# Offsets of three rounds found in their own partitions, keys ahead of the early edge blocks, large searches moved into the rounds, x loaded behind the first block

## The reference

```python
def _L0_gnn_ref(node_features, edge_features, src, dst, W_node, b_node, W_edge, b_edge, W_msg, b_msg):
    h = node_features @ W_node.T + b_node
    e = edge_features @ W_edge.T + b_edge
    msg = h[src] + e
    msg = msg @ W_msg.T + b_msg
    n = node_features.shape[0]
    s = jax.ops.segment_sum(msg, dst, num_segments=n)
    deg = jax.ops.segment_sum(jnp.ones(dst.shape, msg.dtype), dst, num_segments=n)
    return s / jnp.maximum(deg, 1.0)[:, None]
x = _layernorm(x + _L0_gnn_ref(x, edge_attr_128, src, dst, ...), axis=-1)
```

## Time and profile before

| | |
|---|---|
| three runs, us | 789.67, 792.46, 793.79 (median 792.46) |
| the profiled execution's own time | 798.16 us |
| its span, first to last instruction | 796.4 us |
| mean granted TensorE clock | 0.981 |
| PE busy | 697.5 us, 88% |
| DVE, ACT, POOL busy | 613.5 us, 439.5 us, 258.6 us |
| DMA | 130.48 MB, mean 164 GB/s |

### The profile page before, as it was taken

The page is one execution under the profiler, slowest core; times in us unless marked ns, Lnnn a source line. Parts: engine busy times, 40 slices in busy tenths (PEclk is TensorE's granted clock), DMA queues, the critical chain, the costliest instruction groups (busy, mean ns, idle before and its releaser), DMA issues.

```text
span 796.4 us, 24735 instructions
## 1 busy us (share of the span) xinstructions
PE 697.5 (88%) x10331; PEld 622.1 (78%) x10331; DVE 613.5 (77%) x1120; ACT 439.5 (55%) x902; POOL 258.6 (32%) x205
## 2 busy tenths in 40 slices
PE   2624558999999899999999998999999999999995
PEld 2523446898898678988989887988889988989994
DVE  7507998799988668887888777789788788779822
ACT  4103955576565455655656554655656665656641
POOL 2112742000442714426416437353254443000000
PEclk9999969999999989999999999999999999999998
DMA  6985334363474255565563473744744564554200
GB/s 209 219 261 176 108 109 127 110 229 124 131 246 157 78 188 173 204 193 190 186 203 127 135 246 121 266 150 158 264 147 130 189 215 163 178 178 167 68 15 16
DMA packets 81030, 130.48 MB, mean 164 GB/s; under 512 B 11669, under 2 KB 24688, under 8 KB 80815
## 3 DMA queue, kind: packets, MB, share of 16 engines
q1 hardware_dynamic: 73214, 115.79, 43.9%
q0 software_dynamic: 6976, 12.16, 5.5%
q10 hardware_dynamic: 726, 0.90, 0.5%
HBM read 125.58 MB, written 3.23 MB: 162 GB/s over the span
## 4 chain that ended last, share of the span: by engine, by line
PE 65%; DVE 19%; issue 7%; DMA 4%; SPq 2%; DVEq 1%; another core or an unknown queue 1%; ACT 0%; ACTq 0%
PE x_ps L705 35%; PE count_ps L690 13%; PE win_ps L622 11%; DVE key_hot L841 5%; DVE row_hot L841 4%; PE win_ps L629 2%; DMA edges<-in_edge_attr_dram 2%; DVE onehot L811 2%; SPq L444 1%; PE misc_ps L721 1%; PE misc_ps L722 1%; DVEq L822 1%; DVE x_gathered L936 1%; DVE place L817 1%; DVE sums_e L831 1%
## 5 line engine op out<-in xcount | busy, mean ns | idle before, releaser
L1327 ACT CAST region<-count_ps 128x490 bf16<-128x490 f32 x575 | 324.0, 574 | 191.0 <-PE count_ps L690 169.9
L705 PE MATMUL x_ps<-region,x_rest 128*128 128x250 bf16 x2254 | 411.8, 269 | 0.3
L705 PE MATMUL x_ps<-region,x_hi 128*128 128x250 bf16 x1127 | 305.3, 271 | 1.7 <-issue 1.5
L565 POOL DMA_INDIRECT x_gathered<-in_x_dram,x_index x144 | 192.5, 1337 | 283.8 <-PE count_ps L690 255.8
L841 DVE TENSOR_TENSOR row_hot<-iota_bf,row 125x3200 bf16<-125x3200 bf16 x115 | 211.5, 1839 | 49.4 <-PE count_ps L690 31.4
L690 PE MATMUL count_ps<-key_hot,row_hot 125*128 125x98 bf16 x2875 | 224.0, 209 | 26.4 <-DVE key_hot L841 16.0
L690 PEld LDWEIGHTS count_ps<-key_hot,row_hot 125*128 125x128 bf16 x2875 | 185.0, 99 | 49.6 <-DVE key_hot L841 19.0
L705 PEld LDWEIGHTS x_ps<-region,x_rest 128*128 128x128 bf16 x2254 | 210.7, 98 | 16.4 <-issue 0.6
L841 DVE TENSOR_TENSOR key_hot<-iota_bf,key 125x2500 bf16<-125x2500 bf16 x115 | 168.6, 1466 | 0.0
L622 PE MATMUL win_ps<-edges,onehot 128*32 128x128 f32 x3232 | 120.5, 294 | 32.6 <-DMA edges<-in_edge_attr_dram 16.4
L622 PEld LDWEIGHTS win_ps<-edges,onehot 128*32 128x32 f32 x3232 | 94.5, 117 | 53.8 <-issue 45.9
(11 more groups left out here) (178 smaller groups left out, 370.8 us busy)
## 6 DMA issues: line engine op xcount, KB each, us to landing
edges<-in_edge_attr_dram SPq DMA_DIRECT2D x101, 1024.0 KB
resid<-in_x_dram SPq DMA_DIRECT2D x25, 125.0 KB
out_dram<-y SPq DMA_DIRECT2D x25, 125.0 KB
x_gathered<-in_x_dram,x_index POOLq DMA_INDIRECT x144
region<-in_dst_dram ACTq DMA_DIRECT2D x1, 768.0 KB
win_src<-in_src_dram,clipped_int POOLq DMA_INDIRECT x23, 3.4
x_index<-in_src_dram SPq DMA_DIRECT2D x9, 8.0 KB, 6.3
region<-in_L_gnn_W_node_dram SPq DMA_DIRECT2D x1, 64.0 KB
```

The source lines that it names most:

```text
L565: pool.indirect_dma_start(out=x_gathered[:, i, :], out_offset=None, in_=x[:, :], in_offset=bass.IndirectOffsetOnAxis(ap=x_index[:, k, i:i ...
L705: mm = pe.matmul(x_ps[m % 2][:, 0:NB], rows, counts[m % 2][:, b, :], start=(n == 0), stop=(n == PARTS - 1))
L1327: act.copy(counts[m % 2][:, :, f * FILL * 2:(f + 1) * FILL * 2], count_ps[fill % COUNT_BANKS][:, 0:FILL * KEYS].rearrange("p (n b) -> p b ...
```

## The change

`LEAD` falls from 8 to 5; the three edge blocks that leave the early slots are put into the rounds, which hold them in pairs. The offsets of rounds 0, 1 and 2 are found apart from the jobs (`NEAR` = 3): for each, GpSimd gathers a window of 275 entries a partition (`load_near`), three counts of 188, 224 and 260 entries (`find_near`) give the starts of the partition's own two nodes and of the next one, and `take_slots` uses them where they are, without DRAM and without a transpose. Two jobs remain: 0 (30 nodes a partition, rounds 3 to 17) and 1 (14 nodes). Their windows are gathered once `begin_job` has run in segments 0 and 1, job 0 is searched in segments 4 to 6 and job 1 in 7 and 8. `make_keys(0)` stands ahead of the sums of early block 1, the first one-hots of a segment behind those sums. The weights' products move from segments 0 to 2 to segments 2 and 3, and degrees and checks move later. SP waits for all of `dst` before the first edge block, then issues block 0, the first 21 of 49 pieces of x, waits for the window of round 0 (`near_in[0]`), then issues the rest of x and only then edge block 1. `copy_hi` stands behind the windows of block 0. GpSimd's splits of x are put between its gathers. The last 1584 columns of `sums_e` hold job 0's window and are zeroed in segment 9. Each round finds its way through the rest of the program as before.

```diff
-LEAD = 8
+LEAD = 5
...
-JOBS = 3
+JOBS = 2
+NEAR = 3
+NEAR_L = 275
...
-    JOB_K = (5, 31, 14)
-    JOB_N = (N0, N0 + PB * JOB_K[0], 0)
-    JOB_L = (375, 1375, 750)
-    JOB_DVE = (3, 13, 4)
-    JOB_ROWS = (2, B_ROUNDS - 2, G0 - GX)
-    JOB_ROUND = (0, 2, B_ROUNDS)
...
+    JOB_K = (30, 14)
+    JOB_N = (N0 + NEAR * NB, 0)
+    JOB_L = (1375, 750)
+    JOB_DVE = (13, 4)
+    JOB_ROWS = (B_ROUNDS - NEAR, G0 - GX)
+    JOB_ROUND = (NEAR, B_ROUNDS)
...
-    SLOTS_B, SLOTS_A, DEGREES = 5, 8, 8
+    SLOTS_B, SLOTS_A, DEGREES = 9, 17, 13
...
-            def load_x():
-                sp.wait_ge(x_zeroed, 1)
-                whole = N // P
-                sp.dma_start(x_rest[:, 0:whole, :], x[0:whole * P, :].rearrange("(b p) d -> p b d", p=P)).then_inc(x_in_dram, 16)
-                sp.dma_start(x_rest[0:N - whole * P, whole, :], x[whole * P:N, :]).then_inc(x_in_dram, 16)
+            def load_x(i):
+                whole, half = N // P, 21
+                if i == 0:
+                    sp.dma_start(x_rest[:, 0:half, :], x[0:half * P, :].rearrange("(b p) d -> p b d", p=P)).then_inc(x_in[0], 16)
+                else:
+                    sp.wait_ge(x_zeroed, 1)
+                    sp.dma_start(x_rest[:, half:whole, :], x[half * P:whole * P, :].rearrange("(b p) d -> p b d", p=P)).then_inc(x_in[1], 16)
+                    sp.dma_start(x_rest[0:N - whole * P, whole, :], x[whole * P:N, :]).then_inc(x_in[1], 16)
 
...
+            sp.wait_ge(dst_in, 48)
             for t in range(NS):
                 load_edges(t)
+                if t == 0:
+                    load_x(0)
+                    sp.wait_ge(near_in[0], 16)
+                    load_x(1)
                 if t == 3:
-                    load_x()
-                if t == 6:
                     load_small()
...
-            for k in range(JOBS):
-                load_job(k)
-            for m in range(2):
-                load_window(m)
-            for i in range(7):
+            load_near(0)
+            split_rest(0)
+            split_rest(1)
+            load_window(0)
+            load_near(1)
+            for i in range(2, 5):
                 split_rest(i)
-            for i in range(7):
+            load_window(1)
+            load_near(2)
+            for i in range(5, 7):
+                split_rest(i)
+            load_job(0)
+            for i in range(3):
+                split_low(i)
+            load_window(2)
+            load_job(1)
+            for i in range(3, 7):
                 split_low(i)
...
-                    if t in (0, 1):
-                        pe.wait_ge(count_taken, t + 1)
-                        count_blocks(t + 1)
-                    if t == 4:
-                        turn_slots(0)
                     place_windows(u)
-                    if t == 6:
+                    if t == 0:
+                        pe.wait_ge(count_taken, 2)
+                        count_blocks(2)
+                    if t == 1:
                         turn_keys(0)
                     continue
...
-                    if f == 4 and g == 0:
+                    if f == 1 and g in (0, 1):
+                        pe.wait_ge(count_taken, NEAR + g)
+                        count_blocks(NEAR + g)
+                    if f == 0 and g == 2:
                         turn_weights()
-                    if f == 4 and g == 1:
+                    if f == 4 and g == 2:
                         make_weights()
...
+            def find_near(r):
+                dve.wait_ge(near_in[r], 16)
+                for i in range(3):
+                    hi = NEAR_HIGH[0] * i + NEAR_HIGH[1]
+                    nodes[0] += 1
+                    if nodes[0] > 2:
+                        dve.wait_ge(node_counted, nodes[0] - 2)
+                    dve.tensor_scalar(dve_junk[nodes[0] % 2][0:PB, 0:hi], win_near[r][0:PB, 0:hi], near_node[r][:, i:i + 1], None, ALU.is_lt, ALU.add,
+                                      accum_out=near_cnt[r][:, i:i + 1]).then_inc(node_counted, 1)
+                dve.wait_ge(node_counted, nodes[0])
+                link(dve.tensor_scalar(near_start[r][:, :], near_cnt[r][:, :], near_base[r][:, 1:2], None, ALU.add))
+                take_slots(r, 1, near_start[r][:, :].rearrange("p (i g) -> p i g", g=1))
...
-            ins.then_inc(rel_ready, 1)
-            begin_job(0)
-            block_counts(1)
+                ins.then_inc(rel_ready, 1)
+                if q == 1:
+                    begin_near(0)
...
+            make_place(0)
+            dve.wait_ge(rel_copied, 2)
+            make_onehot(0)
+            find_near(0)
...
+            begin_near(1)
...
-                if u < LEAD:
-                    if t in (0, 1):
-                        begin_job(t + 1)
-                    if t == 1:
-                        count_nodes(0, 0, JOB_DVE[0])
-                        end_job(0)
-                    if t == 2:
-                        check_sorted()
-                    if t == 3:
-                        check_job(0)
-                    if t == 4:
-                        make_slots(0)
-                    if t == 6:
-                        make_keys(0)
+                if t == 1:
+                    begin_near(2)
+                    block_counts(3)
+                    check_sorted()
+                    make_keys(0)
...
-                if u == LEAD - 1:
+                if u == 1:
+                    find_near(1)
                     make_hots(0)
+                if u == 3:
+                    find_near(2)
...
-                    if s == (2 if m == 1 else 1) and m + 1 < ROUNDS:
+                    if s == (2 if m == 2 else 1) and m + 1 < ROUNDS:
                         make_keys(m + 1)
-                    if g < 3:
-                        count_nodes(1, [0, 4, 9][g], [4, 9, 13][g])
                     if g == 0:
+                        begin_job(0)
+                        block_counts(4)
+                    if g == 1:
+                        begin_job(1)
+                    if g == 2:
                         dve.wait_ge(wm_turned, 1)
...
-                    if g == 2:
-                        end_job(1)
+                    if g == 3:
                         copy_weights()
                         dve.sem_inc(early_done, 1)
-                    if g == 4:
-                        count_nodes(2, 0, JOB_DVE[2])
-                    if g == 5:
-                        make_slots(1)
-                        end_job(2)
-                    if g == SLOTS_A:
-                        make_slots(2)
+                    if 4 <= g < 7:
+                        count_nodes(0, [0, 4, 9][g - 4], [4, 9, 13][g - 4])
+                    if g == 7:
+                        end_job(0)
+                        count_nodes(1, 0, JOB_DVE[1])
+                    if g == 9:
+                        make_slots(0)
+                        end_job(1)
...
-            act.copy(sums_e[:, :], zero_col[:, 0:1].to_broadcast([P, SE_COLS])).then_inc(zeroed, 1)
+            act.copy(sums_e[:, 0:SCRATCH], zero_col[:, 0:1].to_broadcast([P, SCRATCH])).then_inc(zeroed, 1)
...
+                    if t == 0:
+                        for i in range(7):
+                            copy_hi(i)
                     if t == 1:
-                        sign_counts(0, JOB_DVE[0], JOB_K[0])
-                    if t == 2:
-                        send_starts(0)
-                    if t == 3:
-                        fetch_starts(0)
-                    if t >= 5:
-                        copy_hi(t - 5)
-                    if t == 6:
                         spread_keys(0)
...
-                if g < 2:
-                    for i in range(3 + 2 * g, 5 + 2 * g):
-                        copy_hi(i)
-                if g < 3:
-                    sign_counts(1, [13, 19, 25][g], [19, 25, 31][g])
-                if g == 3:
+                if 4 <= g < 7:
+                    sign_counts(0, [13, 18, 24][g - 4], [18, 24, 30][g - 4])
+                if g == 7:
+                    send_starts(0)
+                    send_near()
+                    sign_counts(1, JOB_DVE[1], 9)
+                if g == 8:
+                    fetch_starts(0)
+                    sign_counts(1, 9, JOB_K[1])
+                if g == 9:
+                    act.wait_ge(starts_ready[0], 1)
+                    act.copy(sums_e[:, SCRATCH:SE_COLS], zero_col[:, 0:1].to_broadcast([P, SE_COLS - SCRATCH])).then_inc(zeroed, 1)
+                if g == 10:
                     send_starts(1)
-                if g == 4:
+                if g == 11:
                     fetch_starts(1)
-                    sign_counts(2, JOB_DVE[2], 9)
-                if g == 5:
-                    sign_counts(2, 9, JOB_K[2])
-                if g == 6:
-                    send_starts(2)
-                if g == 7:
-                    fetch_starts(2)
                     fetch_chunks()
```

181 lines of the change are left out of this document (115 added, 66 removed).

## The result

| | before | after |
|---|---|---|
| median of 6 runs each, same chip | 791.56 us (789.54 to 793.79) | 785.90 us (783.87 to 787.45) |
| ratio, 95% interval | | 0.9925 (0.9898 to 0.9952) |
| profiled execution: own time, span | 798.16, 796.4 us | 783.87, 782.0 us |
| first product with x | 116.38 | 97.08 |
| x sums 0, 1, 2 taken | 150.33, 177.57, 206.68 | 138.39, 172.19, 198.70 |

I had forecast 765 us and a range of 752 to 782: the sign was right, the size far off, and the time lies outside the range. The table's last two rows say where to look. At the first product 19.3 us are gained, not 35.4. At x sum 0 11.9 are left, at x sum 1 5.4.

What follows compares the result with a forecast made beforehand. TensorE's own work was taken to bound the rounds from round 1, and waits for edge rows and VectorE the start. Start -35.4, edge blocks +3.8, round 1 +4 gave -27.6: 770.6 us profiled, 765 median, range 752 to 782.

Steps and rivals of the forecast that it cites:

- The order of events up to edge block 1: Start: near window lands at about 19.5 us, rest of x issued at 19.6, block 1 there at 31 to 33.
- The second condition: Start: the first product with x also needs all of GpSimd's splits, forecast done at 75 to 79 us.
- Rival (b): Start gains only half: block 1 at 42 us, first product at 92 to 97, time 779 (776 to 787); chance 0.18.
- I add 2 us: Round 0: VectorE time lost to GpSimd's splits, taking VectorE's 79 us for the first product to 81.
- upper bound of 95: First product at latest 95 us: block 1 at 38, every lower split fully in VectorE's way, both chains waiting in turn.
- Round 1, 38 us: Round 1 with the moved search work takes 38 us instead of 34.0, a term of +4.
- Round 2, nothing added: Round 2 gets no added term; the old kernel's 27.2 us a round stays.
- lie under TensorE's work: Zeroing of 1584 columns, take_slots for three rounds and later checks are hidden in the rounds; uncovered, 3 us.
- Rival (e): Slower: TensorE's clock at its lower level in rounds 1 and 2 adds 43.6 us, time 808; chance 0.04.
- +3.8 for three edge blocks: Rounds behind the first product: three more edge blocks at 1.28 us each cost 3.8 us.
- From the trace to the median: Whole kernel: the median lies 5.7 us under the profiled execution, as before, so 770.6 becomes 765.
- The 0.92 for faster: Whole kernel: chance of 0.92 that it gets faster by more than 4 us.

Runs made afterwards that it cites:

- e1: Kernel after with GpSimd's 14 splits of x cut to one column and the lower parts of x left out; ratio to before 0.9833, first product 86.61 us.
- e11: Kernel after with splits cut as in e1, the big searches' windows fetched early and index loads later; ratio to before 0.9655, first product 77.36 us.
- e13: Kernel after with the big searches' windows fetched early and index loads later, splits left on GpSimd; ratio to before 0.9955, first product 94.68 us.
- e4: Kernel after with all 14 splits of x made by VectorE instead of GpSimd; ratio to before 0.9874, first product 95.04 us.
- e7: Kernel of e4 with SP's index loads later, behind edge blocks 10 to 14; ratio to before 0.9831, first product 91.38 us.
- e5: Kernel after with ScalarE's send of starts behind segment 8's first bank copy and the degree rows made one segment earlier; ratio to before 0.9861.
- e10: Kernel of e7 with search windows early, signs in segments 1 to 6, send behind a bank copy, degree rows and copy before one-hots; ratio to before 0.9740.
- e6: Kernel after with eight early edge blocks instead of five (LEAD = 8); ratio to before 0.9999, first product 104.32 us.
- e16: Kernel after, unchanged, profiled again and timed on a second chip; ratio to before 0.9968, first product 96.59 us.

## Why the prediction was wrong

**The order of events up to edge block 1**: right. Near window, second part of x, block 1 at 31.11 for 31 to 33 (my own terms with 9.1 us for x add up to 33.8, not 33). The second condition, all splits done at 75 to 79, was met only at 85.33, but it was not what the product waited for: at 97.08 that was a bank copy behind VectorE's one-hots. Rival (b) expected the start to gain only half, and it did (19.3 of 35.4), but its mechanism, block 1 at 42, was not what happened.

**"I add 2 us"** is the term that failed. I had one row for it, a placing matrix of 1.69 us, and named GpSimd's 28.3 us of splits, of which half should lie under a wait for edges. Of the first seven only two ran in that wait; three stood beside the block counts at 30, two beside a placing matrix at 50, and they lengthened VectorE's rows by 8.6 us. The lower splits lengthened them by 10.8. The splits cost the first product 10.5 us as the kernel stands and 17.3 with the queue free (e1, e11, e13). The prediction's upper bound of 95 had only the lower ones fully in the way; the measured 97.08 is above it. The Trainium skill's page SBUF — State Buffer (section "SBUF: two separate sides") says that the port pair shared by GpSimd and some VectorE operations is an exclusive lock, and that a DMA issued by GpSimd waits while VectorE holds it. The trace agrees in both directions: 7.72 for 2.24 us, and a gather of 5.92. By that rule all 15.2 us of the lower splits could stand before VectorE, and that was nearer than my 2.

**Round 0's edge rows**: not in the prediction. I removed the 16.4 us wait of the earlier trace rows and noted that GpSimd's queue had moved 1.06 MB in it, but didn't ask where these bytes would go. They went to 70 to 86 us, together with two edge blocks of round 0, which then took 16 to 18 us from issue to use (e1, e4, e7). The bunching costs 2.4 us now and 9.3 once VectorE is faster (e13, e11).

**TensorE's clock in the start**: not in the prediction, which asked for it in rounds 1 and 2 alone. In the trace of after it was at 0.50 from about 73 to 93 us, from within a wait of 4.13 us on and through one of 8.46, and VectorE then waited 2.18 us for keys that TensorE had turned at 90.07. In e11 it was there only from about 67 to 74 us. So some of what the splits cost came by way of the clock; how much, no run separates.

**Round 1, 38 us**: 41.3. The signs and counts fitted (36.3 in e5); the 5.0 us that e5 took off again are the send ahead of the bank copies. **Round 2, nothing added**: 33.8 against 27.2, of which 4.5 us are from the degree rows (a wait of 3.24 us), the keys behind them and the clock (e10). I had written that later steps "lie under TensorE's work", and bounded them at 3 us. Rival (e) had the clock right in kind: it was at its lower level for some 7 and 3.5 us behind two waits, not for two rounds.

**+3.8 for three edge blocks**: 3.4 (e6), within what traces of one chip differ by.

**From the trace to the median.** I took the profiled execution of before 5.7 us above its median, and carried this over. After's lay 2.0 below. That is 7.6 us of the miss of 20.9; the other 13.3 are in the trace (783.87 for 770.6). And these 13.3 owe something to luck. The start came 16.1 us later than forecast, rounds 1 and 2 took 3.3 and 6.6 more, together 26.0. The stretch behind them gave 12.8 back, 10.0 of them from x sum 2 to the last: 573.3 us where 579.5 and 3.8 made 583.3. No term of mine says so; the first trace of before was slow there, and in e16 the same stretch took 585.5. What sets this spread between chips and executions is open. In the first trace of before TensorE stood in holes of 1 us in its window sums at 275 to 282 us that the profile puts down to nothing ("issue"), while the DMA moved 47 GB/s; I made no experiment on it. The 0.92 for faster came true on the first chip (5.7 us); the second, with 0.3%, lies within what I had called no change. The range held no term for this spread, and its upper end stopped in the middle of rival (b).

## What to carry to other kernels

Work on GpSimd is not free where VectorE is the bound: count every microsecond of it that overlaps VectorE as VectorE's, until a row shows otherwise, and compare with making it on VectorE itself (25.6 us on one, 14.8 on the other here). When transfers are moved out of a wait, ask which wait they will be in next, and look for a stretch in which the DMA moves nothing. Before a slow issue is blamed for a wait, find out which transfer the wait was for: count back by the slots, and split rows that join several issues. An engine's queue that holds a send which waits for another engine holds everything behind it: put such a step behind the copies that others wait for. And test two suspected causes in all four combinations, since each can hide the other. A forecast against one profiled execution should carry a term for how much two traces of one kernel differ, here up to 12 us between chips.

## What the runs showed of the hardware

Steps of VectorE of 0.3 to 2.2 us took up to 7.72 us beside GpSimd's subtractions (that one ended 2.1 us behind the last of three), and GpSimd's gather of the first big search's windows took 5.92 us beside VectorE's block counts and one-hots of 2-byte words, which kept their 2.24 and 1.82 us, and 2.69 in e11. A subtraction of 896 columns of float32 took 1.9 us on GpSimd and 1.05 on VectorE. An index load of 8 KB took 8.5 to 9.3 us to issue on SP while GpSimd's windows of 1.06 MB and two edge blocks were in the DMA queues, and an edge block of 1 MB took 16 to 18 us from issue to use there. TensorE, granted its upper level before, was granted 0.50 behind single waits of 3.24 and 4.53 us. The same kernel after took 573.3 and 585.5 us for the same twenty rounds in two traces, the second on a chip where the kernel before is slower too.
